# Sorted experts in three routed groups, laid over the rotary, tile and wide stages, with second weights read at a register's offset

## The reference, cut to what matters

```python
attn_out = ao @ Wo + bo
x1 = _layernorm(x + attn_out, g1, be1)
gate_probs = softmax(x1 @ Wg + bg)
topk_p, topk_i = top_k(gate_probs, 2)
topk_p = topk_p / sum(topk_p)
comb = sum(one_hot(topk_i, 8) * topk_p[..., None], axis=-2)
h = gelu(einsum('bsd,edf->bsef', x1, W1) + b1, approximate=False)
y = einsum('bsef,efd->bsed', h, W2) + b2
moe_out = einsum('bse,bsed->bsd', comb, y)
return _layernorm(x1 + moe_out, g2, be2)
```

## Time and profile before

| | us |
|---|---|
| median of three runs | 5848.35 |
| the profiled execution's own time | 5848.49 |
| its span | 5846.5 |
| TensorE busy | 5225.1 (89%) |
| VectorE busy | 4051.5 (69%) |
| ScalarE busy | 2679.7 (46%) |
| GpSimd busy | 1214.1 (21%) |
| mean granted TensorE clock | 0.936 of full |

### The profile page before, as it was taken

One profiled execution on the slowest core, in us unless ns is written; L12 is line 12 of the kernel. 1 busy time (PEld: TensorE's weight loads), 2 busy tenths in 40 slices (PEclk: granted clock), 3 DMA queues, 4 the chain that ended last, 5 costly groups with the idle time before them and its releaser, 6 DMA issues. The chain is left out here.

```text
span 5846.5 us, 85273 instructions
## 1 busy us (share of the span) xinstructions
PE 5225.1 (89%) x31156; PEld 2620.0 (45%) x31156; DVE 4051.5 (69%) x7021; ACT 2679.7 (46%) x4489; POOL 1214.1 (21%) x859
## 2 busy tenths in 40 slices
PE   6999997787999999989999928489999999997999
PEld 2333333344567777762222227333433433434676
DVE  7888885774677777769899723677677777763412
ACT  4656665221233333337777805244444444442333
POOL 0110100220122222311210042233334334341000
PEclk7999998787999999999999959799999999998999
DMA  4211110001111111102122022100000000001000
GB/s 87 46 31 30 33 28 11 0 0 57 36 39 26 29 25 29 35 11 39 34 33 36 11 74 65 29 24 12 12 12 16 9 12 16 12 12 37 4 4 8
DMA packets 145923, 155.38 MB, mean 27 GB/s; under 512 B 48612, under 2 KB 92692, under 8 KB 145092
## 3 DMA queue, kind: packets, MB, share of 16 engines
q1 hardware_dynamic: 140904, 140.84, 11.4%
q0 software_dynamic: 4096, 8.40, 0.5%
q10 hardware_dynamic: 504, 0.69, 0.1%
HBM read 117.13 MB, written 36.49 MB: 26 GB/s over the span
## 5 line engine op out<-in xcount | busy, mean ns | idle before, releaser
L3802 DVE TENSOR_REDUCE wide_max_parts<-wide_p 128x2 f32<-128x1024 f32 x496 | 596.0, 1220 | 139.9 <-PE wide_p L3771 127.4
L732 ACT ACTIVATE attn_w<-l_p 128x512 f32<-128x512 f32 x1024 | 549.3, 597 | 277.6 <-DVE l_p L1176 153.8
L2490 PE MATMUL caus_p<-caus_x_one,big 128*128 128x129 f32 x4608 | 639.9, 286 | 0.0
L583 DVE TENSOR_REDUCE l_max_parts<-l_p 128x2 f32<-128x1024 f32 x512 | 602.1, 1219 | 45.8 <-PE l_p L559 41.4
L2574 ACT ACTIVATE big<-caus_p 128x512 f32<-128x512 f32 (+3 forms) x768 | 344.9, 489 | 573.5 <-PE caus_p L2476 419.4
L2490 PEld LDWEIGHTS caus_p<-caus_x_one,big 128*128 128x128 f32 x4608 | 590.7, 198 | 36.0 <-issue 2.5
L583 DVE TENSOR_REDUCE rot_max_parts<-rot_p 128x2 f32<-128x1024 f32 x488 | 574.2, 1219 | 46.4 <-PE rot_p L559 44.2
L4054 PE MATMUL wide_p<-wide_q,wide_k 64*128 64x512 f32 x2048 | 530.4, 596 | 0.0
L4182 ACT ACTIVATE attn_w<-wide_p 128x1024 f32<-128x1024 f32 x342 | 350.1, 1024 | 356.5 <-PE wide_p L4054 352.9
L3988 POOL TENSOR_TENSOR big<-big,attn_w 128x1024 f32<-128x1024 f32 x128 | 330.1, 2579 | 419.0 <-PE wide_p L3771 407.3
L583 DVE TENSOR_REDUCE caus_max_parts<-caus_p 128x2 f32<-128x1024 f32 (+2 forms) x360 | 340.6, 957 | 24.2 <-PE caus_p L559 15.9
(11 more groups left out here) (598 smaller groups left out, 8812.5 us busy)
## 6 DMA issues: line engine op xcount, KB each, us to landing
pair_q_stack<-q_parts SPq DMA_DIRECT2D x576, 32.0 KB
pair_k_stack<-k_parts SPq DMA_DIRECT2D x576, 32.0 KB
wide_inverse<-inverse_rows SPq DMA_DIRECT2D x64, 256.0 KB
l_q_stack<-q_parts SPq DMA_DIRECT2D x279, 32.0 KB
l_k_stack<-k_parts SPq DMA_DIRECT2D x279, 32.0 KB
big<-in_L_ffn_W SPq DMA_DIRECT2D x32, 256.0 KB, 6.2
q_parts<-pair_parts_q SPq DMA_DIRECT2D x8, 768.0 KB, 3.6
k_parts<-pair_parts_k SPq DMA_DIRECT2D x8, 768.0 KB, 3.6
```

Of the source, the lines that this page charges most:

```text
L583: self.nc.vector.tensor_reduce(self.max_parts[:, 2 * p:2 * p + 2, n, half], pair[:, :, 0:self.width(n, half)], AX.X, ALU.max).then_inc(*se ...
L732: self.nc.scalar.activation(self.exps[t % len(self.exps)], bank, ACT.Exp).then_inc(*self.exped.up())
L2490: mm = nc.tensor.matmul(outs[o % 2][:, nq % 2 * (C + 1):(nq % 2 + 1) * (C + 1)], exps[h % 2][:, kb, nq * P:(nq + 1) * P], x_one[b % 2][:, ...
L3802: self.nc.vector.tensor_reduce(self.max_parts[:, :, n, h], side, AX.X, ALU.max).then_inc(*self.maxed.up())
```

## The change

- **Three groups.** `ROUTED` has group 0 with tiles 0 to 15 (batches 0 and 1), group 1 with 16 to 23 and group 2 with 24 to 31. They have 39, 23 and 23 sorted tiles, 85 in all instead of 78.
- **Group 0 in the rotary stage.** `finish` of batch 1's last unit gets the logits, 13 slots of gate pieces, the counts, 6 slots of place pieces and 32 slots with one scatter each. The loads of expert weights (24 DMAs on SP's queue) hang on `finish` of units 12 and 13. They go to `arena`, the room that the stacks, values and parts of the attention before it used.
- **Groups 1 and 2 beside tiles.** `beside[J]` lists what is laid beside tile J: for group 1 logits and pieces from J = 0, counts at 9, places from 10, scatters from 14, for group 2 the same 14 tiles later. GpSimd waits for `up` of the tile ahead before each scatter or gather.
- **Gathers.** Group 0 is gathered from J = 42, one indirect DMA per tile, combined at 53, 61, 69 and 77; batch 0's tail begins at 62, and `early` at 74, two per tile. Groups 1 and 2 are gathered and combined (chunks of two tiles) in the wide stage, and the tails of batches 1, 2 and 3 run there too. The first seven wide units take three more steps of `later` each, eight in all.
- **Weights.** The copy of a tile's weights has 516 columns, b1 and W1. `down` reads an offset register by `value_load` on TensorE and takes W2 from `arena` at that register's offset.
- Names moved without a change in what they do: `Tail`, `Gathered`, `SortedStart`; `big` shrinks and several buffers share `arena`.

```diff
+ROUTED = ((0, 16), (16, 8), (24, 8))
+PER_EXPERT = FF // P + 2 * FF
...
+def tiles_for(n):
+
+    return (2 * n * P + E2 * (P - 1)) // P
...
+    def scatter_on_pool(self, pool, new, s, n):
+        if new(self.core.moe_in_cleared, 16 * len(ROUTED)):
+            pool.wait_ge(*self.core.moe_in_cleared.at(16 * len(ROUTED)))
+        if new(self.placed, 1):
+            pool.wait_ge(*self.placed.at(1))
+        self.nc.gpsimd.indirect_dma_start(
+            self.core.moe_in[self.g][:, :], self.place_of(s, n), self.core.x_mid[:, self.first_tile + n, :],
+            None).then_inc(*self.scattered.up(16))
+
...
+        self.st = st = Stage(core, "sort")
+        self.nc, self.inp = core.nc, core.inp
+        self.gates = st.sbuf("gates", [P, core.n_batch * NT, E2])
+        self.router = Router(st, E2)
+        rooms = [core.big[:, 0:2 * T]] + [core.attn_w[:, 3 * BANK:4 * T]] * 2
+        self.routes = [Route(st, g, self.router, rooms[g], self.gates) for g in range(len(ROUTED))]
+        self.routes[2].fixed_loaded = self.routes[1].fixed_loaded
+        self.w = core.arena[:, 0:E2 * PER_EXPERT].rearrange("p (e w) -> p e w", e=E2)
+        self.w_loaded = st.sem("expert_w_loaded")
...
+    def expert_on_sp(self, e):
+        b, w1 = FF // P, FF // P + FF
+        for dst, src in ((self.w[:, e, 0:b], self.inp["L2_ffn_b1_c"][:, e, :]),
+                         (self.w[:, e, b:w1], self.inp["L2_ffn_W1"][e]),
+                         (self.w[:, e, w1:].rearrange("p (c d) -> p c d", d=C),
+                          self.inp["L2_ffn_W2"][e].rearrange("(c p) d -> p c d", p=P))):
+            self.nc.sync.dma_start(dst, src).then_inc(*self.w_loaded.up(16))
 
 
...
         b, g = units[u]
+        if u in (len(units) - 4, len(units) - 3):
+            half = u - len(units) + 4
...
+                 [("turn", 2 * b)], [("turn", 2 * b + 1)]]
+        if NT * (b + 1) == route.first_tile + route.n:
+            pieces = [("gate_piece",)] * Route.GATES
+            pieces[Route.BEFORE_EXP:Route.BEFORE_EXP] = [("route_exp",)]
+            places = [("place_piece",)] * Route.PLACES
+            steps += [[("logits",)]] + [pieces[i:i + 2] for i in range(0, len(pieces), 2)] + [[("counts",)]]
+            steps += [places[i:i + 2] for i in range(0, len(places), 2)]
+            steps += [[("scatter", s, n)] for n in range(route.n) for s in range(2)]
+        return steps
...
                     proj.split_on_sp(sp, *args)
+                elif kind == "expert":
+                    e = args[0]
+                    proj.stored_on_sp(sp, new, nb - 1)
+                    if e < E2 // 2:
+                        n = PairWeighted.PER_UNIT * (len(units) - 2)
+                        if new(heads.scored, n):
+                            sp.wait_ge(*heads.scored.at(n))
+                    sort.expert_on_sp(e)
...
-        at = v.value_load(self.routes.offset[0:1, g, js[i]:js[i] + 1], min_val=0, max_val=(E2 - 1) * PER_EXPERT)
-        self.nc.vector.tensor_copy(self.current[J % 4][:, :],
-                                   self.core.big[:, bass.ds(at, PER_EXPERT)]).then_inc(*self.copied.up())
+        at = v.value_load(route.offset[0:1, js[i]:js[i] + 1], min_val=0, max_val=(E2 - 1) * PER_EXPERT)
+        self.nc.vector.tensor_copy(self.current[J % 4][:, 0:self.CHUNKS + FF],
+                                   self.core.arena[:, bass.ds(at, self.CHUNKS + FF)]).then_inc(*self.copied.up())
...
+        route, js = self.quads[Q]
+        at = pe.value_load(route.offset[0:1, js[i]:js[i] + 1], min_val=0, max_val=(E2 - 1) * PER_EXPERT)
...
-                                       self.current[J % 4][:, first:first + P], start=c == 0,
+                                       self.core.arena[:, first:][:, bass.ds(at, P)], start=c == 0,
...
+class Gathered:
+
+
+
+    def __init__(self, st, routes, room, size, first, last, tag):
+        self.st, self.nc, self.core, self.size = st, st.nc, st.core, size
+        self.chunks = [(route, at) for route in routes[first:last] for at in range(0, route.n, size)]
+        self.room = room.rearrange("p (b s n c) -> p b s n c", b=2, s=2, c=C)
+        self.gathered = [st.core.new_sem() for _ in range(2)]
+        self.half_combined, self.combined = st.sem(f"half_combined{tag}"), st.sem(f"combined{tag}")
+
+    def on_pool(self, pool, c, s, i):
+        route, at = self.chunks[c]
+        if c >= 2 and s == 0 and i == 0:
+            pool.wait_ge(*self.combined.at(self.size * (c - 1)))
+        self.nc.gpsimd.indirect_dma_start(
+            self.room[:, c % 2, s, i, :], None, self.core.moe_out[route.g][:, :],
+            route.place_of(s, at + i)).then_inc(*self.gathered[c % 2].up(16))
+
+    def on_dve(self, v, c):
+        route, at = self.chunks[c]
+        first = route.first_tile + at
+        acc = self.core.x_mid[:, first:first + self.size, :]
+        v.wait_ge(*self.gathered[c % 2].at(32 * self.size * (c // 2 + 1)))
+        for s, (m, done) in enumerate(((route.top.m1, self.half_combined), (route.top.m2, self.combined))):
+            if s:
+                v.wait_ge(*self.half_combined.at(self.size * (c + 1)))
...
+    def steps(self, b):
+        return [("tail", kind, b) for kind in ("stats_1", "root_1", "scale_1", "by_gamma", "plus_beta", "plus_x",
+                                               "stats_2", "root_2", "scale_2")] + [
+            ("tail_turn", c) for c in range(HALF * b, HALF * (b + 1))]
...
+    beside = [[] for _ in range(len(tiles) + LAG)]
+
+    def lay(first, steps, at_once=1):
+
+        for i, step in enumerate(steps):
+            beside[min(first + i // at_once, len(beside) - 1)].append(step)
+
+    for g, first in ((1, 0), (2, 14)):
+        route = routes[g]
+        pieces = [("gate_piece", g)] * Route.GATES
+        pieces[Route.BEFORE_EXP:Route.BEFORE_EXP] = [("route_exp", g)]
+        lay(first, [("logits", g)] + pieces, 3)
+        lay(first + 9, [("counts", g)])
+        lay(first + 10, [("place_piece", g)] * Route.PLACES, 3)
+        lay(first + 14, [("scatter", g, s, n) for n in range(route.n) for s in range(2)])
+    for c, first in enumerate((3, 7, 11, 15, 33, 37, 49, 53)):
+        lay(first, [("gate_row", c), ("none",), ("biases", c)])
+    done = routes[0].n_out + LAG
+    lay(done + 1, [("gather", c, s, i) for c in range(len(back.chunks)) for s in range(2)
+                   for i in range(back.size)])
+    for c in range(len(back.chunks)):
+        lay(done + 2 * back.size * (c + 1) + 4, [("combine", c)])
+    first = done + 2 * back.size * 2 + 5
+    steps = tail.steps(0)
+    lay(first, steps + [("narrow",)])
+    lay(first + len(steps) + 1, early, 2)
...
-                if kind == "scatter":
-                    routes.scatter_on_pool(pool, *args)
+                if kind == "up":
+                    J = args[0]
+                elif kind == "scatter":
+                    g, s, n = args
+                    if new(experts.up_mm, J):
+                        pool.wait_ge(*experts.up_mm.at(J))
+                    routes[g].scatter_on_pool(pool, new, s, n)
...
-    work, later = [], []
+    work, later = [], tail.steps(1)
+    for b in range(2, nb):
+        chunks = [c for c, (route, at) in enumerate(back.chunks) if (route.first_tile + at) // NT == b]
+        later += [("gather", chunks[0])]
+        for c in chunks:
+            later += [("gather", c + 1)] if c < chunks[-1] else []
+            later += [("none",), ("combine", c)]
+        later += tail.steps(b)
...
+            if u < PAIRS - 1 and kb in (1, 3, 5):
+                plan += next_later()
...
+                elif kind == "gather":
+                    c = args[0]
+                    for s in range(2):
+                        for n in range(back.size):
+                            back.on_pool(pool, c, s, n)
```

798 lines of the change are left out of this document (406 added, 392 removed).

## The result

The changed kernel took 5798.52 us (median of 4 runs, 5794.54 to 5807.32) against 5847.04 for the kernel before, measured beside it (4 runs, 5843.68 to 5861.05): ratio 0.9915, 95% interval 0.9894 to 0.9935. It is 48.5 us faster; 108 were forecast. The time lies inside the range given, at its upper end.

The account below looks back on a forecast made before the run. TensorE, 89% busy, bounds the kernel except in the 432.2 us expert stage; saving 206 less 30, 4, 4, 10 gives 158, less rotary 30 and wide 20 is 108: 5848.5 to 5740 us, own range 5710 to 5775, over cases 5670 to 5800.

Parts of the forecast that it names:

- Entry, tiles, the tail gone: Expert stage: 6 us to the first `up` against 71, 74 tiles in 152 us, no 89 us tail.
- Register on TensorE: Expert stage: a `value_load` before each `down` costs 0.4 us for 74 tiles, 30 us (0 to 63).
- Copies: Expert stage: VectorE's weight copies fall from 0.70 to 0.37 us; 4 us added for tiles behind a combine or norm.
- Paced DMAs: Expert stage: 64 scatters and gathers, one per tile, cost 10 us (0 to 44).
- Rotary: Rotary stage: logits 3.5, routing 8 and bursts 18 us, together a cost of 30.
- The routing's term: Rotary stage: group 0's routing overfills VectorE's slots by 0.5 us each; cost 8 us (4 to 13).
- The burst's term: Rotary stage: two bursts of group 0's scatters, 26 and six, cost 18 us (0 to 37).
- Wide: Wide stage: tails and combines fit VectorE's free time, delayed maxima 12, turns 2.6, gathers 5; cost 20 us (8 to 50).
- VectorE becomes the bound: Rival, rotary and wide stages: routing and tails paid in full, 13.5 + 60 us; 5793 us, chance 0.09.
- The register load is dear: Rival, expert stage: register load costs 0.85 us or more per tile, no cover; 5780 to 5800 us, chance 0.15.
- Cover everywhere: Rival, all stages: register load hidden, paced DMAs free, rotary scatters half price, 6 less in wide; 5685 us, chance 0.25.
- An indirect DMA stops code at any pace: Rival, slower case: 64 tiles lose 2.5 us each, rotary 45, wide 53; 5965 us, chance 0.06.

Follow-up runs that it names:

- Pacing: Changed kernel, GpSimd waiting before each of the 32 rotary scatters for its slot's scores: 5771.01 us, ratio 0.9867, first chip.
- the adds placed: Changed kernel, GpSimd's adds also waiting for the VectorE combine or tail piece ahead of them: 5731.27 us, ratio 0.9920, second chip.
- the meetings gone from both kernels: GpSimd's adds wait for all VectorE pieces: changed kernel, scatters also paced, 5704.47 us (0.9873); kernel before 5752.53 us (0.9954).
- the spread pace: Changed kernel with paced scatters, adds behind all VectorE pieces, and fewer later steps at a time in the wide stage: 5692.53 us, ratio 0.9856.
- the copies: Changed kernel, VectorE again copying all 1028 weight columns and TensorE reading the copy without a register load: 5779.40 us, ratio 1.0004.
- both remedies: Changed kernel with scatters paced by the scores and GpSimd's adds behind VectorE's combine and tail pieces: 5727.69 us, ratio 0.9908.
- the control: The changed kernel run again unaltered on the third chip: 5765.66 us, ratio 0.9980.

## Why the prediction was wrong, step by step

*Entry, tiles, the tail gone*: right. Entry 7.24 us (forecast 6), no stretch without tiles. *Register on TensorE*, forecast 30 us (0 to 63): at most 0.06 x 74 = 4, near the end "full cover". VectorE's 0.75 us did not carry over to TensorE. *Copies*: 0.43 us each in the median (forecast 0.37). *Paced DMAs*, forecast 10: from 45 to 125 us into the stage there were 264 products of `up` on the first chip and 278 on the third, by the changed kernel's groups by line:

```profile
L3439 PE MATMUL moe_p<-big 128*128 128x128 f32 x264 | 35.9, 279 | 3.2 <-DVE big L3427 2.9 <-issue 0.3
...
L3439 PE MATMUL moe_p<-big 128*128 128x128 f32 x278 | 37.6, 278 | 1.5 <-DVE big L3427 1.5
```

The 14 products are 1.75 tiles of 2.16 us, so 3.8 us, less than half of the forecast, if the paced DMAs are what the chips differ by there. The stage came to 255.9 us where the sum had 274; with the register's term at 0 the sum had been 244, 12 short, which was not followed up.

*Rotary*, forecast 30, measured 52.9. The logits' 3.5 measured 3.7. The routing's term of 8 (4 to 13) measured 11.6 in the three half units that hold it. It was priced as VectorE's overflow, but TensorE is busy 7 us longer there without the logits, and idle 4 us longer: most of the cost went by at the lower clock, which the term did not hold. The burst's term of 18 (0 to 37) measured 35.0, in three bursts where two were foreseen: the mechanism as argued, the size low; the stalls are followed by products at half clock. Pacing gave back 33.1 of it. 2.8 us more lie in two half units ahead of the routing, with the clock at 0.97 and 0.91.

*Wide*, forecast 20 (8 to 50), measured 73. This is the step that failed: "In sum they fit. [...] I take 12." The work was forecast well (60 us; VectorE's busy time without the meetings rose by 279.6 - 218.1 = 61.5) and it did fit in sum, with 303.4 - 218.1 = 85 us idle. The idle share did not help: the 61.5 us cost 37 with the adds placed (340.4 against 303.4, across two chips) although VectorE had room. A piece stands ahead of the maxima in its queue, and TensorE waits for them (7.27 us on VectorE's maxima in the timeline above, 50 in the groups by line). That these 37 come from the place in the queue is argued from those waits; no run tested it by itself. The sum had no term for GpSimd at all: the meetings with GpSimd's adds cost 36 to 41 more, by 34 us of VectorE lengthened. Part of both is TensorE's clock: the granted clock was 0.95 in these units, so some of their time went by at 1.2 GHz, where the kernel before had 0.99, 2.4 GHz nearly throughout; TensorE was busy 19 us longer for 24 products more. The gathers' 5 us were 0.

The 12 came from a row at 94% busy in the earlier trace rows, laid over an average. The units one by one hold a like piece, the first batch's closing, whose work on VectorE is a tail and its rows. It made its four units 7.1 + 12.1 + 2.7 + 2.8 = 24.7 us longer in the kernel before. Three times that is 74, close to the 73 measured, but this is luck. The windows of four plain units and of these four show why:

```profile
3990.20:4164.80 174.60, 174.41 (x902) 63.87 (x904) 127.00 (x120) 85.14 (x85) 69.87 (x28) 1.00 0.05 13
4164.80:4364.27 199.47, 193.41 (x1054) 81.53 (x1056) 146.24 (x199) 86.35 (x87) 71.88 (x28) 0.99 0.05 12
```

TensorE is busy 19.0 us longer there, with 152 products more: the closing's own projection, logits and turns, 17.8 us in the groups by line. A tail has 8 turns alone. What is left is some 7 us for 19 us of VectorE's work, so 21 for three, and the trace before held no price near 73. The runs show what was new, the meetings above all and then the density of the pieces: with the meetings gone from both kernels the change costs the wide stage 33.3 us, and 23.6 with the spread pace, near the 20 forecast.

*The rivals.* "VectorE becomes the bound" (5793, 0.09) came nearest, by 5.5 us, in part by luck: VectorE was not full in the wide stage (310 of 376 us), it was blocked and in the way, and the routing did not cost its 13.5 us in rotary but 11.6, mostly as TensorE's clock. "The register load is dear" (5780 to 5800, 0.15) fits the total and is refuted by the copies. "Cover everywhere" was right of the register alone. "An indirect DMA stops code at any pace" fell with the paced scatters, on the chip where bursts do starve. The rule of the Trainium skill weighed there ("Runtime: NRT & Kernel Launch", section "Instruction fetch mechanics", crossing a block of code mostly hidden) agrees with the traces of three of the five chips under the same bursts and with the total on a fourth, and not with those of the chip that the forecast was for.

## What to carry to other kernels

Free time on an engine is not room: VectorE had 85 us idle in seven units, and 61.5 us of work cost 73. Before pricing added work by what a like piece costs in the same loop, take out what that piece costs on the bounding engine itself, and look at what the added pieces will meet. Where GpSimd and VectorE both work on SBUF, look for one source line with two durations, and let GpSimd wait for the piece, so that it runs beside a reduction from PSUM: that wait gave 41 us with the tails and 27 with the closings. Pace indirect DMAs by a semaphore of the engine that they run beside, since it cost nothing here and the bursts cost 35 us on one chip and nothing on the others.

## What the runs showed of the hardware

The same program differs by 1.2% between chips (5847 to 5849 and 5776 to 5778 us), for the kernel before all of it, where both kinds were profiled, in the stage with bursts of back-to-back indirect DMAs. The DMA view of the changed kernel lists the queues that share the 16 engines (packets, MB, share):

```profile
q0 software_dynamic: 4096, 8.40, 0.5%
q8 instruction: 250, 4.10, 0.3%
```

If that queue carries the code, it comes in packets of 4.10 MB / 250 = 16.4 KB, and both queues are nearly idle on average; whether they get in each other's way, and why on one chip alone, stays open. A register load on TensorE and products at its address cost at most 0.06 us a tile. A VectorE operation of 0.16 us takes 2.3 us if GpSimd's add of 2.8 us has begun. The same rotary code took 803.9 to 812.7 us in different executions on chips of one kind, and most of that is TensorE's clock. Its windows around the logits, in the kernel with both remedies and in the control:

```profile
3054.31:3089.14 34.83, 34.83 (x176) 11.72 (x175) 23.94 (x34) 18.49 (x35) 6.94 (x6) 0.80 0.25 51
3056.30:3086.40 30.10, 30.10 (x177) 9.95 (x175) 23.88 (x33) 18.48 (x35) 6.97 (x6) 0.94 0.24 52
```

TensorE is busy all the time in both and makes the same products. Behind the 32 narrow products of the logits (128x8) it ran at 1.2 GHz, for 11 us in the first (eight products for the values in 1.94 us, 1.07 elsewhere) and for under 4 us in the second. What decides between the two courses is not shown. The expert stage's 249.4 to 258.4 us go with the clock in the same way, as told above.
